# GpSimd writes and gathers scratch rows by index beside the experts of a cross-attention and mixture-of-experts layer

## The chip, the cores and the metric

One core of one Trainium2 chip. The metric is the time of the device for one execution in microseconds (us). Engines are named as in the profile: PE is TensorE (with PEld its weight loads), DVE VectorE, ACT ScalarE, POOL GpSimd, SP SyncE; a "q" behind a name is that engine's sequencer where it issues transfers.

## The reference, cut to what matters

Eight batches of 512 rows of 256 numbers go through two parts, each added to its input:

```python
x = x + xattn(ctx, layernorm(x), mask, ...)      # 8 heads of 32
x = x + ffn(layernorm(x), ...)
# ffn: 16 experts, the best 8 of a row by a gate, and a shared one
logits = l2norm(xf) @ l2norm(gate_w).T
combine = top-8 of sigmoid(logits), divided by their sum
y = (silu(xf @ w_gate[e]) * (xf @ w_up[e])) @ w_down[e]      # for each e
out = sum over e of combine[:, e] * y  +  (silu(xf @ sw_gate) * (xf @ sw_up)) @ sw_down
```

## The kernel before

The first part (attention) runs over 16 groups of 4 heads. The second part, which the change touches, runs over 8 x 17 units: for each batch b, the 16 experts e = 0 to 15 and the shared one as e = 16. All are computed for all rows. Numbers are split in a high and a low half, and each product is three matmuls.

**One order for all engines.** A list `ORDER` of steps is made before anything is built. Each engine's program walks the whole list and issues what is its own of each step, so the list is each engine's order; semaphores do the rest. The second part of the list is written by `order()`. For unit n = (b, e) it holds, in this order:

- in batch 0 only, `split_w` of a later expert (ACT rounds the weights to the high half at L866, POOL subtracts for the low half at L1429 and L1431). The weights of expert e + 2 are split ahead of unit e;
- `load_c`, which SP issues (L641): the combine weights of an expert, broadcast from a DRAM scratch to the tile `cb`, four buffers;
- `gate_up` (12 matmuls on PE), `silu` (ACT: `sg`), `unit` (DVE: `qb`, L1300 and L1311), `hi_h` (ACT: `hh`), `lo_h` (DVE: `hl`, L1316);
- what the next batch needs (below);
- `down` of unit n - 2 (6 matmuls on PE into `pst`).

**What the next batch needs.** At e = 0 to 6 of batch b five steps at a time of the chain `ln2` of batch b + 1 are put in. Its 33 steps are: statistics of the rows on DVE (steps 0 to 7: `st`, `mv`), two small ones on POOL (8 and 9: `ve`, L1358 and L1360), two on DVE (10 and 11: the first guess of a reciprocal root, L1067 and L1069), seventeen small ones on POOL (12 to 28, L1362 to L1378, the last writes `rn`), and four copies on ACT (29 to 32) that write the normalised rows into the tile `xm` (`XM`, 128 x 4 x 256). Step 29 lies at e = 5, steps 30 to 32 at e = 6. ACT waits ahead of step 29 until POOL has finished step 28. At e = 7 and e = 8 PE transposes `xm` (`turn_x2`, L665; four transposes each), and ACT and DVE split the result into the two halves that the units of batch b + 1 read. The gating follows at e = 10 to 13.

ACT, DVE and POOL run strictly in the list's order, so an ACT that waits at step 29 holds back the `silu` of unit e = 6 and all behind it. There is one `xm`.

In batch 0, POOL's splits of experts 9 to 16 fall beside units e = 7 to 14. PE's `gate_up` of an expert waits for its split.

Of the kernel before, what the change touches and what calls it, by code (L numbers as in the profile page):

```python
# [6 lines left out]
F32 = mybir.dt.float32  # L7
F32R = mybir.dt.float32r
I32 = mybir.dt.int32
# [4 lines left out]
B, S, D, F = 8, 512, 256, 512  # L14
# [34 lines left out]
N_TANH = 5  # L49


TODO = [(b, e) for b in range(B) for e in range(E + 1)]


# [180 lines left out]
def order():  # L235


    def chain(name, count, *key):
        return [(name, *key, i) for i in range(count)]

    out = attention()

    def run(c, k=None):
        k = len(c) if k is None else min(k, len(c))
        out.extend(c[:k])
        del c[:k]

    cb, split = FIRST_UNITS + NC, NEARLY
    turned = {0}
    tail = []  # L250

    def load_c(upto):
        nonlocal cb
        while cb < min(upto, B * E) and cb // E in turned:
            out.append(("load_c", cb))
            cb += 1

    c = []
    for n in range(FIRST_UNITS, len(TODO) + LAG):
        b, e = TODO[min(n, len(TODO) - 1)]  # L260
        if n < len(TODO):
            if b == 0:
                while split < min(e + 3, E + 1):
                    out.append(("split_w", split))
                    split += 1
            load_c(b * E + min(e, E) + NC)
            out += [("gate_up", n), ("silu", n), ("unit", n), ("hi_h", n), ("lo_h", n)]
            if b + 1 < B:
                if e == 0:
                    c = chain("ln2", N_LN2, b + 1)  # L270
                if e < 7:
                    run(c, 5)
                if e in (7, 8):
                    out.append(("turn_x2", b + 1, e - 7))
                if e == 10:
                    c = chain("gating", N_GATE, b + 1)
                if 10 <= e < 13:
                    run(c, 7)
                if e == 13:
                    run(c)  # L280
                    out.append(("turn_c", b + 1))
                    turned.add(b + 1)
            if tail and e in (3, 4):
                out.append(("store", tail[0], e - 3))
                if e == 4:
                    tail.pop(0)
        if n >= LAG:
            out.append(("down", n - LAG))
            if TODO[n - LAG][1] == E:
                tail.append(TODO[n - LAG][0])  # L290
    out += [("store", B - 1, 0), ("store", B - 1, 1)]
    return out


ORDER = order()


# [47 lines left out]

def build(nc, x, ctxT, mask, WsT, bs_k, bs_v, WtT, bt, WoT, bo, gate, wg, wu, wd, ident, out):
    cscr = nc.dram_tensor("combine_scratch", (B, 2 * E, 2, 4, 32), F32, kind="Internal").ap()
    with ExitStack() as top:
        made = {}

# [94 lines left out]
        assert place[0] + NEARLY * 24 * D <= late_at, "and these on the last group's"  # L445
        WX = s2("weights2", [128, E + 1, 6 * D], F32R)
        YT = s2("yt", [128, 2, S])
        OB = s2("ob", [128, 2, 2, D])
        GUh, GUl = (WX[:, :, 512 * n:512 * n + 512].rearrange("p e (a k h) -> p e a k h", a=2, k=2) for n in range(2))
        DNh, DNl = (WX[:, :, 1024 + D * n:1024 + D * n + D] for n in range(2))  # L450
# [101 lines left out]
        def sync_program(engine):  # L552
# [96 lines left out]
            for half in range(2):  # L649
                sp.wait_ge(sem(f"st_out{half}"), 16 * B)  # L650
            sp.wait_ge(sem("st_ct"), 64 * B)

        def tensor_program(engine):
            pe = Waiter(engine)
# [207 lines left out]
        def scalar_program(engine):  # L862
# [5 lines left out]
            for step in ORDER:  # L868
# [115 lines left out]
                elif step == ("grows", N_GROWS - 1):  # L984
                    act.wait_ge(sem("gate_t"), 1)
                    gb = bank(step)[:, 0:2 * E].rearrange("p (k e) -> p k e", k=2)
                    four = gb.rearrange("p k (f e) -> p k f e", f=1).to_broadcast([128, 2, 4, E])
                    copy(GT[:, :, :, 0, :], four).then_inc(sem("gate_hi"), 1)
                elif kind == "second_starts":
                    act.wait_ge(sem("ctx_lo"), 4 * B)  # L990
                    act.wait_ge(sem("q_lo"), NG)
                    act.wait_ge(sem("k_lo"), NG)
                    act.wait_ge(sem("v_f"), 2 * B)
                    act.wait_ge(sem("k"), NG)
                    act.wait_ge(sem("y_add"), COUNT["out_y", B - 1, 0, 1])
                    act.wait_ge(sem("x_bo"), B)
                elif kind in ("early_w", "split_w"):
                    e = step[1]
                    act.wait_ge(*w_loaded(e))
                    if FIRST_W <= e < NEARLY:  # L1000
                        act.wait_ge(*place_free(e))
                    copy(GUh[:, e].rearrange("p a k h -> p (a k) h"), WR[:, e % NR, 0:4, :]).then_inc(sem("w_hi"), 1)
                    copy(DNh[:, e, :], WR[:, e % NR, 4:6, :].rearrange("p a b -> p (a b)")).then_inc(sem("w_hi"), 1)
                elif kind == "ln2" and step[2] >= N_SMALL2:
                    _, b, i = step
                    q = i - N_SMALL2
                    act.wait_ge(sem("ln2"), N_SMALL2 * (b + 1))
                    if b > 0:
                        act.wait_ge(sem("x2_t"), 2 * b)
                    else:  # L1010
                        act.wait_ge(sem("x_t"), 2 * B)
                    copy(XM[:, q, :], X1[:, 4 * b + q, :], ACT.Identity, bias=NMR2[:, q:q + 1], scale=RS2[:, q:q + 1]).then_inc(
                        sem("xm"), 1)
                elif kind == "turn_x2":
                    _, b, j = step
                    act.wait_ge(sem("x2_t"), 2 * b + j + 1)
                    if b >= 2:
                        act.wait_ge(sem("gu"), 2 * 17 * (b - 1))
                    copy(X2h[:, b % 2, j, :], bank(step)).then_inc(sem("x2_hi"), 1)
                elif kind == "gating" and step[2] == N_TANH:  # L1020
                    b = step[1]
                    act.wait_ge(sem("gating"), N_GATE * b + 5)
                    act.wait_ge(sem("ln2"), N_SMALL2 * (b + 1))
                    for q in range(4):
                        copy(SC[:, q, :], LG[:, q, :], ACT.Tanh, scale=RN[:, q:q + 1]).then_inc(sem("tanh"), 1)
                elif kind == "first_ends":
                    act.wait_ge(sem("av"), 2 * NG)
                    act.wait_ge(sem("u_norm"), NG)
                    act.wait_ge(sem("y_add"), COUNT["out_y", B - 1, 1, 1])
                    act.wait_ge(sem("ut_lo"), NG)  # L1030
                elif kind == "silu":
                    n = step[1]
                    if n == 0:
                        for z in range(2):
                            for h in range(4):
                                act.wait_ge(sem(f"stack{z}{h}"), 96 * B)
                    act.wait_ge(sem("gu"), 2 * n + 1)
                    if n >= 2:
                        act.wait_ge(sem("hq"), n - 1)
                    if n < TANH_UNITS:  # L1040
                        copy(SG[:, n % 2, :], GP[n][0], ACT.Tanh, scale=0.5).then_inc(sem("silu"), 1)
                    else:
                        copy(SG[:, n % 2, :], GP[n][0], ACT.Silu).then_inc(sem("silu"), 1)
                elif kind == "hi_h":
                    n = step[1]
                    b, e = TODO[n]
                    if e < E:
                        act.wait_ge(sem("hc"), b * E + e + 1)
                    else:
                        act.wait_ge(sem("hq"), n + 1)  # L1050
                    if n >= NH:
                        act.wait_ge(sem("dn"), n - NH + 1)
                    copy(HHB[:, n % NH, :], QB[:, n % 2, :]).then_inc(sem("h_hi"), 1)
                elif kind == "down":
                    b, e = TODO[step[1]]
                    if e == E:
                        act.wait_ge(sem("dn"), step[1] + 1)
                        if b > 0:
                            act.wait_ge(sem("y_t"), 2 * b)
                        copy(YT[:, 0, :], YP[:, 0, :]).then_inc(sem("yt0"), 1)  # L1060

# [273 lines left out]
        def gpsimd_program(engine):  # L1335
            pool = Waiter(engine)

            for step in ORDER:
# [79 lines left out]
                elif kind == "second_starts":  # L1418
                    pool.wait_ge(sem("k"), NG)
                    pool.wait_ge(sem("v_f"), 2 * B)  # L1420
                    pool.wait_ge(sem("y_add"), COUNT["out_y", B - 1, 0, 1])
                elif kind in ("early_w", "split_w"):
                    e, i = step[1], W_AT[step[1]] - 1
                    if FIRST_W <= e < NEARLY:
# [51 lines left out]
```

## Time and profile before

| | |
|---|---|
| median of 2 runs | 1054.62 us (1053.51 to 1055.73) |
| the profiled execution's own time | 1049.61 us |
| its span in the profile | 1047.5 us |
| PE busy | 1003.0 us (96%) |
| DVE busy | 655.4 us (63%) |
| ACT busy | 467.2 us (45%) |
| POOL busy | 389.4 us (37%) |
| DMA, mean | 84 GB/s |

The first part and the second meet between 430 and 475 us; from there on the profile is eight times the same stretch. A share of busy time of the whole span mixes both. The times of one batch are read from the timeline, where two equal instructions of two batches lie a batch apart.

### The profile page before, as it was taken

Reading aid. Unit: us, or ns where it says so; the run is one execution under the profiler, and the core shown is the slowest. Engines: PE = TensorE matmul, PEld = TensorE weight load, DVE = VectorE, ACT = ScalarE, POOL = GpSimd, SP = SyncE. Lnnn points to the kernel's source line nnn. Section 1 sums busy time; section 2 is a strip of 40 time slices with the busy share of each in tenths; the row PEclk is TensorE's granted clock in tenths of the full one; section 3 lists DMA queues with packets and bytes.
Section 4 is the critical chain, followed back from the end, with each engine's and each line's share of the span. In section 5 each row is a group of like instructions: output and inputs, shape, how many; then the busy total and the mean of one; then the engine's idle time right before and its main releaser. Section 6 shows DMA issues by size and latency. Waiting matters only on the chain.

```text
span 1047.5 us, 14744 instructions
## 1 busy us (share of the span) xinstructions
PE 1003.0 (96%) x5070; PEld 761.4 (73%) x5070; DVE 655.4 (63%) x1510; ACT 467.2 (45%) x881; POOL 389.4 (37%) x355
## 2 busy tenths in 40 slices
PE   4889999999999998899999999999999999999998
PEld 3656767676767664567888888888888888888886
DVE  6866767776767577445665566556556556555544
ACT  3447565666565646445424333333333333333322
POOL 2569797879797967345310010010010100100000
PEclk9999999999999997999999999999999999999999
DMA  7543342424242223325333232242341232332230
GB/s 232 131 132 93 101 132 67 128 72 134 70 114 70 65 64 101 81 81 122 95 72 68 52 81 58 54 82 50 63 80 42 71 82 46 74 75 60 67 72 24
DMA packets 84377, 87.87 MB, mean 84 GB/s; under 512 B 13160, under 2 KB 66296, under 8 KB 84304
## 3 DMA queue, kind: packets, MB, share of 16 engines
q1 hardware_dynamic: 82384, 84.85, 32.9%
q10 hardware_dynamic: 1920, 2.10, 0.6%
q8 instruction: 40, 0.66, 0.3%
q14 instruction: 33, 0.27, 0.1%
HBM read 56.99 MB, written 4.46 MB: 59 GB/s over the span
## 4 chain that ended last, share of the span: by engine, by line
PE 89%; DVE 5%; ACT 2%; SPq 1%; issue 1%; POOL 1%; DMA 1%; DVEq 0%; ACTq 0%; POOLq 0%
PE ps L659 49%; PE pst L659 18%; PE ps L765 5%; PE ps L738 5%; PE pst L754 5%; PE ps L665 4%; DVE mx L1196 1%; PE ps L778 1%; SPq L611 1%; SPq L546 1%; ACT e_buf L866 1%; DVE lg L1277 1%; ACT ctx_h L866 0%; DVE wsrc_l L1145 0%; DMA x<-in_x 0%
## 5 line engine op out<-in xcount | busy, mean ns | idle before, releaser
L659 PE MATMUL ps<-x_h,weights 128*128 128x512 f32 x1088 | 365.6, 397 | 2.8 <-DVE sg L1297 2.0
L659 PEld LDWEIGHTS ps<-x_h,weights 128*128 128x128 f32 x1088 | 204.4, 188 | 52.7 <-issue 2.5
L1196 DVE TENSOR_REDUCE mx<-ps 128x1 f32<-128x512 f32 x256 | 173.2, 684 | 95.4 <-PE ps L738 94.8
L659 PE MATMUL ps<-x_l,weights 128*128 128x512 f32 x544 | 214.5, 394 | 0.0
L866 ACT ACTIVATE hh<-qb 128x512 fp32r<-128x512 f32 x136 | 86.0, 632 | 287.7 <-DVE qb L1311 268.2
L659 PE MATMUL pst<-hh,weights 128*128 128x512 f32 x544 | 193.2, 397 | 0.0
L866 ACT ACTIVATE e_buf<-pst 128x512 f32<-128x512 f32 x256 | 147.1, 595 | 100.4 <-PE pst L754 90.5
L1300 DVE TENSOR_TENSOR qb<-ps,sg 128x512 f32<-128x512 f32 x136 | 94.0, 691 | 135.9 <-PE ps L659 132.2
L1316 DVE TENSOR_TENSOR hl<-qb,hh 128x512 fp32r<-128x512 f32 x136 | 94.3, 693 | 92.2 <-ACT hh L866 92.0
L1406 POOL TENSOR_TENSOR e_sums<-e_sums,e_buf 128x1024 f32<-128x1024 f32 x60 | 143.4, 2390 | 8.6 <-ACT e_buf L866 2.5
L1358 POOL TENSOR_SCALAR ve<-mv 128x4 f32<-128x4 f32 x8 | 1.8, 229 | 337.8 <-DVE mv L1238 337.8
L738 PE MATMUL ps<-k_stack,q_stack 97*128 97x512 f32 x256 | 109.8, 431 | 11.3 <-DVE mx L1196 9.1
L659 PEld LDWEIGHTS ps<-x_l,weights 128*128 128x128 f32 x544 | 102.1, 188 | 24.9
L659 PEld LDWEIGHTS pst<-hh,weights 128*128 128x128 f32 x544 | 102.1, 188 | 24.0 <-DVE hl L1316 0.8
L754 PE MATMUL pst<-q_stack,k_stack 98*128 98x512 f32 x256 | 108.2, 424 | 10.3 <-ACT e_buf L866 10.2
L866 ACT ACTIVATE sg<-ps 128x512 f32<-128x512 f32 x136 | 80.9, 595 | 74.6 <-PE ps L659 73.6
L659 PE MATMUL pst<-hl,weights 128*128 128x512 f32 x272 | 107.5, 395 | 0.0
L1406 POOL TENSOR_TENSOR e_sums<-e_buf 128x1024 f32<-128x1024 f32 x30 | 71.8, 2395 | 50.3 <-PE ps L778 50.0
L1311 DVE TENSOR_TENSOR qb<-qb,cb 128x512 f32<-128x512 f32 x124 | 87.8, 708 | 4.2
L738 PEld LDWEIGHTS ps<-k_stack,q_stack 97*128 97x128 f32 x256 | 49.2, 193 | 52.4 <-issue 32.3
L754 PEld LDWEIGHTS pst<-q_stack,k_stack 98*128 98x128 f32 x256 | 49.3, 193 | 25.5 <-ACT e_buf L866 17.3
L765 PE MATMUL ps<-e_buf,v_buf 128*32 128x512 f32 x512 | 65.1, 628 | 0.0
(154 smaller groups left out, 1360.7 us busy)
## 6 DMA issues: line engine op xcount, KB each, us to landing
cb<-combine_scratch SPq DMA_DIRECT2D x128, 256.0 KB, 4.7
q_stack<-q_h SPq DMA_DIRECT2D x128, 64.0 KB, 2.0
k_stack<-k_h SPq DMA_DIRECT2D x124, 64.0 KB, 2.0
ctx_raw<-in_ctxT SPq DMA_DIRECT2D x7, 1024.0 KB, 5.3
q_stack<-q_l SPq DMA_DIRECT2D x64, 64.0 KB, 2.0
out_x<-ob SPq DMA_DIRECT2D x16, 256.0 KB, 2.1
k_stack<-k_l SPq DMA_DIRECT2D x62, 64.0 KB, 2.0
x<-in_x SPq DMA_DIRECT2D x7, 512.0 KB, 6.8
```

The lines of the kernel that those rows point to most:

```text
L546: e.dma_start(f32(KS[g % 2][at:at + 32, h, :]), f32(src[32 * h:32 * h + 32, :])).then_inc(sem(f"stack{g % 2}{h}"), 16)
L659: ins = engine.matmul(dst, lhsT, rhs, start=start and n == 0, stop=stop and n == len(terms) - 1)
L665: ins = engine.transpose(dst, src, ID[0:k, 0:k])
L738: engine.matmul(ps, QS[z][0:97, h, 128 * q:128 * q + 128], KS[z][0:97, h, :], start=True, stop=True).then_inc(sem("s_max"), 1)
L754: engine.matmul(YP[:, m % 2, :], KS[z][0:98, h, 128 * k:128 * k + 128], QS[z][0:98, h, :], start=True, stop=True).then_inc(sem("s_t"), 1)
L765: ins = engine.matmul(OP[32 * i:32 * i + 32, :], VB[:, b % 2, k, hh + i, :], EB[:, SLOTS[8 * g + 4 * (i // 2) + k], i % 2, :], start=k == ...
L866: return engine.activation(dst, src, func, **kw)
L1196: engine.tensor_reduce(MX[:, g % 2, h // 2, h % 2, q:q + 1], bank(step), AX.X, ALU.max).then_inc(sem("max"), 1)
L1300: engine.tensor_tensor(QB[:, w, :], GP[n][1], SG[:, w, :], ALU.mult).then_inc(sem("hq"), 1)
L1311: engine.tensor_tensor(QB[:, w, :], QB[:, w, :], CB[:, m % NC, :], ALU.mult).then_inc(sem("hc"), 1)
L1316: engine.tensor_tensor(HLB[:, n % NH, :], QB[:, w, :], f32(HHB[:, n % NH, :]), ALU.subtract).then_inc(sem("h_lo"), 1)
L1406: engine.tensor_tensor(ES[:, a, :, :], first, EB[:, SLOTS[n + 1 + i], :, :], ALU.add).then_inc(sem("e_add"), 1)
```

## The change

A DRAM scratch `routed_rows` of 4096 rows of 256 numbers, a tile `ix` with the row numbers (partition p, column c holds 32 p + c) and a tile `gathered` with four buffers are added. POOL gets two kinds of steps:

- `put`: 32 for each batch b + 1, at e = 6 to 13 of batch b, four in each unit. Each is an indirect DMA that writes 128 rows of `xm` (1 KB each) to the scratch rows named by a column of `ix`; each of the four quarters of `xm` is written eight times. The first waits for the four copies into `xm` and, from the second batch on, until all 32 gathers before have landed.
- `take`: 32 for each batch from 1 on, at e = 0 to 5 of that batch, 6, 5, 5, 6, 5 and 5 of them, behind the `ln2` steps of the same e. Each is an indirect DMA that gathers 128 rows from the scratch into `gathered`. The first waits until all 32 puts have landed; each waits until the take four before it has landed, since it writes the same buffer.

Nobody reads `gathered`. ACT gets one more wait, ahead of step 29: the puts of the batch before must have landed, since the copies write `xm` again. SP waits for the last takes at the end. The 7 batches 1 to 7 have 224 puts and 224 takes in all.

```diff
+PUTS = 32
...
+            if b + 1 < B and 6 <= e < 14:
+                out += [("put", b + 1, 4 * (e - 6) + i) for i in range(4)]
+            if b > 0 and 0 <= e < 6:
+                out += [("take", b, i) for i in range(PUTS) if i * 6 // PUTS == e]
...
+    routed = nc.dram_tensor("routed_rows", (128 * PUTS, D), F32, kind="Internal").ap()
...
+        IX, GB = s2("ix", [128, PUTS], I32), s2("gathered", [128, 4, D])
...
+            for i in range(4):
+                sp.wait_ge(sem(f"take{i}"), 16 * 8 * (B - 1))
...
                     act.wait_ge(sem("ln2"), N_SMALL2 * (b + 1))
+                    if b > 1:
+                        act.wait_ge(sem("put"), 16 * PUTS * (b - 1))
...
+                elif kind == "put":
+                    _, b, c = step
+                    if (b, c) == (1, 0):
+                        pool.wait_ge(sem("dn"), 1)
+                        engine.iota(IX[:, :], pattern=[[1, PUTS]], base=0, channel_multiplier=PUTS).then_inc(sem("ix"), 1)
+                        pool.wait_ge(sem("ix"), 1)
+                    if c == 0:
+                        pool.wait_ge(sem("xm"), 4 * (b + 1))
+                        if b > 1:
+                            for i in range(4):
+                                pool.wait_ge(sem(f"take{i}"), 16 * 8 * (b - 1))
+                    engine.indirect_dma_start(routed, bass.IndirectOffsetOnAxis(IX[:, c:c + 1], 0), XM[:, c // 8, :], None).then_inc(
+                        sem("put"), 16)
+                elif kind == "take":
+                    _, b, c = step
+                    pool.wait_ge(sem("put"), 16 * PUTS * b)
+                    if b > 1 or c >= 4:
+                        pool.wait_ge(sem(f"take{c % 4}"), 16 * (8 * (b - 1) + c // 4))
+                    engine.indirect_dma_start(GB[:, c % 4, :], None, routed, bass.IndirectOffsetOnAxis(IX[:, c:c + 1], 0)).then_inc(
+                        sem(f"take{c % 4}"), 16)
```

POOL's order before, in a batch's chain `ln2`, its first six small steps (`rs`, `rs_a` and `rs_b` are the root's small tiles, `ve` the variances; in brackets the semaphores waited for):

```order
L1358 TENSOR_SCALAR ve<-mv 128x4 [waits xm,tanh,ln2]
L1360 TENSOR_SCALAR ve<-mv 128x4 [waits ln2]
L1362 TENSOR_TENSOR rs_a<-rs 128x8 [waits ln2]
L1364 TENSOR_TENSOR rs_b<-rs_a,ve 128x8 [waits ln2]
L1366 TENSOR_SCALAR rs_b<-rs_b 128x8 [waits ln2]
L1368 TENSOR_TENSOR rs<-rs,rs_b 128x8 [waits ln2]
```

The same place in the changed kernel, batch 1 (its lines stand 11 to 31 further down):

```order
L1369 TENSOR_SCALAR ve<-mv 128x4 [waits tanh,ln2]
L1371 TENSOR_SCALAR ve<-mv 128x4 [waits ln2]
L1451 DMA gathered<-routed_rows,ix 128x256 [waits take2]
L1451 DMA gathered<-routed_rows,ix 128x256 [waits take3]
L1451 DMA gathered<-routed_rows,ix 128x256 [waits take0]
L1451 DMA gathered<-routed_rows,ix 128x256 [waits take1]
L1451 DMA gathered<-routed_rows,ix 128x256 [waits take2]
L1373 TENSOR_TENSOR rs_a<-rs 128x8 [waits ln2]
L1375 TENSOR_TENSOR rs_b<-rs_a,ve 128x8 [waits ln2]
L1377 TENSOR_SCALAR rs_b<-rs_b 128x8 [waits ln2]
L1451 DMA gathered<-routed_rows,ix 128x256 [waits take3]
```

Five takes stand between the first two small steps and the next three; 5, 6 and 5 more stand between the later groups, 21 in all from `ve` to `rn`.

POOL's order before, at the splits of batch 0 (`weights` is the tile with all experts' halves, `w_raw` the loaded weights):

```order
L1429 TENSOR_TENSOR weights_65<-w_raw,weights_65 128x512 [waits w_hi]
L1431 TENSOR_TENSOR weights_65<-w_raw,weights_65 128x256 [waits w_hi]
L1429 TENSOR_TENSOR weights_65<-w_raw,weights_65 128x512 [waits w_hi]
L1431 TENSOR_TENSOR weights_65<-w_raw,weights_65 128x256 [waits w_hi]
L1429 TENSOR_TENSOR weights_65<-w_raw,weights_65 128x512 [waits w_hi]
```

The same place in the changed kernel, from the split of expert 8 to that of expert 10:

```order
L1462 TENSOR_TENSOR weights_65<-w_raw,weights_65 128x256 [waits w_hi]
L1437 IOTA ix 128x32 [waits dn]
L1444 DMA routed_rows<-xm,ix 4096x256 [waits xm,ix]
L1444 DMA routed_rows<-xm,ix 4096x256 x3
L1460 TENSOR_TENSOR weights_65<-w_raw,weights_65 128x512 [waits w_hi]
L1462 TENSOR_TENSOR weights_65<-w_raw,weights_65 128x256 [waits w_hi]
L1444 DMA routed_rows<-xm,ix 4096x256 x4
L1460 TENSOR_TENSOR weights_65<-w_raw,weights_65 128x512 [waits w_hi]
```

Four puts now stand ahead of each of the splits of experts 9 to 16, 32 in all. From batch 1 on the 32 puts stand together on POOL.

## Rows read from the trace of the kernel before

**Rows 1.** The page: busy time by engine; busy tenths, clock and DMA in 40 slices

```profile
PE 1003.0 (96%) x5070; PEld 761.4 (73%) x5070; DVE 655.4 (63%) x1510; ACT 467.2 (45%) x881; POOL 389.4 (37%) x355
...
PE   4889999999999998899999999999999999999998
...
POOL 2569797879797967345310010010010100100000
```

**Rows 2.** Busy time in four stretches of one batch each, all engines

```profile
core 0: us, PE busy (x) PEld busy (x) DVE busy (x) ACT busy (x) POOL busy (x), PEclk, DMA share, GB/s
538.00:612.00 74.00, 74.00 (x328) 59.77 (x327) 43.27 (x91) 25.06 (x46) 4.82 (x20) 1.00 0.31 65
612.00:686.00 74.00, 74.00 (x328) 59.84 (x327) 43.27 (x91) 25.07 (x46) 4.85 (x20) 1.00 0.27 65
```

**Rows 3.** Timeline of POOL, chain ln2 beside batch 2: start, us, instruction, [idle before]

```profile
607.70 0.23 POOL L1358 TENSOR_SCALAR ve<-mv 128x4 f32<-128x4 f32 x1 [64.15 <-DVE mv L1238]
608.01 0.24 POOL L1360 TENSOR_SCALAR ve<-mv 128x4 f32<-128x4 f32 x1
611.88 0.20 POOL L1362 TENSOR_TENSOR rs_a<-rs 128x8 f32<-128x8 f32 x1 [3.63 <-DVE rs L1069]
...
617.28 0.24 POOL L1378 TENSOR_SCALAR rn<-v 128x4 f32<-128x4 f32 x1
681.64 0.23 POOL L1358 TENSOR_SCALAR ve<-mv 128x4 f32<-128x4 f32 x1 [64.12 <-DVE mv L1238]
```

**Rows 4.** Timeline of ACT, the same batch, at e = 5 and 6

```profile
624.11 0.59 ACT L866 ACTIVATE xm<-x,nmr,rs 128x256 f32<-128x256 f32 x1
624.92 0.60 ACT L866 ACTIVATE sg<-ps 128x512 f32<-128x512 f32 x1 [0.22 <-PE ps L659]
...
628.31 1.57 ACT L866 ACTIVATE xm<-x,nmr,rs 128x256 f32<-128x256 f32 x3
```

**Rows 5.** Timeline of PE: the transposes of xm, and where expert 16 of batch 0 begins

```profile
630.32 0.60 PE L665 MATMUL ps<-ident_sb,xm 128*128 128x128 f32 x4
...
519.15 0.40 PE L659 MATMUL ps<-x_h,weights 128*128 128x512 f32 x1
```

**Rows 6.** Timeline of POOL, batch 0: the splits of experts 8 (second half), 9 and 16

```profile
480.12 1.19 POOL L1431 TENSOR_TENSOR weights<-w_raw,weights 128x256 fp32r<-128x256 f32 x1
481.98 1.28 POOL L1429 TENSOR_TENSOR weights<-w_raw,weights 128x512 fp32r<-128x512 f32 x1 [0.66 <-ACT weights L866]
...
515.79 0.75 POOL L1431 TENSOR_TENSOR weights<-w_raw,weights 128x256 fp32r<-128x256 f32 x1
```

**Rows 7.** Groups of POOL by shape, whole run: busy, mean ns, idle before

```profile
L1406 POOL TENSOR_TENSOR e_sums<-e_sums,e_buf 128x1024 f32<-128x1024 f32 x60 | 143.4, 2390 | 8.6 <-ACT e_buf L866 2.5
L1429 POOL TENSOR_TENSOR weights<-w_raw,weights 128x512 fp32r<-128x512 f32 x17 | 21.9, 1287 | 48.5 <-ACT weights L866 48.5
L1431 POOL TENSOR_TENSOR weights<-w_raw,weights 128x256 fp32r<-128x256 f32 x17 | 13.4, 791 | 0.0
```

**Rows 8.** Instructions on the tile cb: SP's issues, ns min, median, max

```profile
L641 SPq DMA_DIRECT2D cb<-combine_scratch x128: 359/360/1393, 425.9 to 1018.5; - x128
```

**Rows 9.** The page: DMA queue of SP, and issues with KB each and us to landing

```profile
q1 hardware_dynamic: 82384, 84.85, 32.9%
...
cb<-combine_scratch SPq DMA_DIRECT2D x128, 256.0 KB, 4.7
...
w_raw<-in_wg SPq DMA_DIRECT2D x17, 128.0 KB, 2.2
```

**Rows 10.** Busy time in stretches of 5 us where PE waits for others

```profile
390.00:395.00 5.00, 3.65 (x17) 2.10 (x15) 2.21 (x5) 3.25 (x7) 4.26 (x11) 0.90 0.38 92
395.00:400.00 5.00, 4.22 (x14) 3.14 (x14) 2.53 (x4) 3.38 (x8) 2.45 (x2) 0.50 0.43 110
```

**Rows 11.** Timelines of POOL and DVE, the same moment

```profile
615.01 0.74 POOL L1366 TENSOR_SCALAR rs_b<-rs_b 128x8 f32<-128x8 f32 x1
...
615.00 0.69 DVE L1316 TENSOR_TENSOR hl<-qb,hh 128x512 fp32r<-128x512 f32 x1 [0.70 <-ACT hh L866]
```

## The prediction

> **What bounds the kernel now.** I read the page's busy times first. PE is busy for 96% of the span and POOL for 37%, but the slices show that POOL's work lies in the first half: from slice 20 on its row reads mostly 0 and 1, and PE's reads 9 but for its last slice [rows 1]. The change lies in that second half, so the mean over the span says nothing of it. The stretches of one batch each do: 74 us long, PE busy for all 74.00, DVE for 43.3, ACT for 25.1, POOL for 4.8 [rows 2]. So one batch is limited by PE alone, and POOL has 69 us of it free. On the share of busy time the change looks free. The timeline has to say whether it is, since POOL's 4.8 us are not just any 4.8 us: they lie in a chain that PE waits for if it is late.
>
> That chain: POOL begins `ve` at 607.70, waits for DVE's first guess until 611.88, and ends `rn` at 617.52. The next batch's `ve` begins at 681.64, so a batch takes 73.94 us [rows 3]. ACT comes to the first copy into `xm` at 624.11, 6.6 us after `rn`: this is all the slack that the chain has. ACT's other three copies end at 629.88 [rows 4], and PE transposes `xm` from 630.32 on [rows 5], 0.44 us later. PE takes its work in order, so every microsecond that `xm` is late beyond that is a microsecond without matmuls.
>
> **What the change puts there.** Nothing is removed. Added are 224 puts and 224 takes, all issued by POOL, 64 in each of the six batches 1 to 6, 32 puts in batch 0 and 32 takes in batch 7. Everything depends on c, the time for which one indirect DMA of 128 rows occupies POOL. The trace of before has no transfer issued by POOL, so c has to be bounded. From below: SP issues a transfer of 256 KB in 0.36 us [rows 8], with nothing but its sequencer at work. From above: a POOL instruction over 128 x 1024 elements, 2.39 us; nearer by are the splits over 128 x 256 and 128 x 512, 0.79 and 1.29 us [rows 7]. [...] I take 1.15 us, between the two splits and nearer to the larger. Below 0.36 us or below nothing I see no reason for it to go: nothing that POOL did before goes away.
>
> *The chain ln2 beside batches 1 to 6.* By the order, 21 takes stand between `ve` and `rn`. POOL's two `ve` end 0.55 us after the start, the 17 small steps take 5.64 us (611.88 to 617.52) [rows 3], and the wait for DVE (3.63 us) is filled by the first five takes if c is over 0.73. So `rn` ends 6.2 + 21c after `ve` began. It may end up to 624.11 - 607.70 = 16.4 us after, and 0.44 us more for PE's slack and some 0.2 for ACT's idle time before `sg` [rows 4, 5]: 17.0. PE loses 21c - 10.8 in each batch; with c = 1.15 that is 13.35, six times 80 us.
>
> *POOL's own round.* In the same batches POOL has 6.2 + 64c, and twice it must wait for landings: the puts for the last take, the takes for the last put. A transfer of 128 KB lands 2.2 us after its issue [rows 9]. 64 x 1.15 + 6.2 + 4.4 = 84.2 us, against 73.9 + 13.35 = 87.3 by the chain. The chain is the longer until c = 1.2; above it POOL sets the pace, with a loss of 64c - 63.3 a batch.
>
> *Batch 0.* Four puts stand ahead of each split of experts 9 to 16. POOL is free at 481.3 (480.12 + 1.19), iota costs some 0.3 and the eight splits 8 x 2.03 (1.28 + 0.75), so that the last ends at 497.8 + 32c. It ended at 516.5 before [rows 6], and PE begins expert 16 at 519.15 [rows 5]. PE loses 32c - 21.3, with c = 1.15 15.5 us. SP, which waits there for POOL's `w_lo` before it loads weights and then `cb`, is behind by the same and not by more.
>
> [...]
>
> *DMA.* The 64 transfers of a batch move 8192 rows of 1 KB. SP's queue had 82384 packets of about 1 KB, which took 32.9% of 16 engines for 1047.5 us, 67 ns each [rows 9]: 8192 x 67 ns / 16 = 34 us a batch, 46% beside the 27 to 31% of before [rows 2]. That stays under 100%, and `cb` is loaded four units ahead of its use (17 us) while it lands in 4.7 [rows 9]. I cost it at nothing; if that cover goes, DVE's `qb` waits. ACT's new wait for the puts is nothing, since POOL gathered after they had landed. The wait of SP at the end is nothing: the takes of batch 7 end 40 us before it.
>
> *POOL beside DVE.* At 615.01 a small step of POOL takes 0.74 us, where its like take 0.20 to 0.24; DVE's subtraction with two inputs in SBUF runs from 615.00 to 615.69 [rows 11]. An indirect DMA that reads `ix` may be held up in the same way. I count this as part of c, since nothing shows it for a transfer. [...]
>
> The row of POOL's splits speaks for a c over 1 us. [...]
>
> Sum: 80 + 15.5 + 15 = 110.5 us on the profiled execution's 1049.6, hence 1160. The median of before lies 5 us above that execution; the same 5 us give 1165.
>
> **Rivals.**
>
> 1. *POOL is occupied for longer and becomes the bound* (c over 1.2). For it: POOL's compute over 1024 elements takes 2.39 us [rows 7], and DVE holds POOL up at times [rows 11]. With c = 1.45: 6 x 29.5 + 25 + 15 = 217 us, 1272. With the upper bound 2.39: 6 x 89.7 + 55 + 15, about 1660. The batch then follows POOL's round and POOL is busy nearly all the time.
>
> 2. *No change: POOL only hands the transfer on.* If c is near SP's 0.36 [rows 8], 21 takes go into the chain's slack. The ring of four buffers then sets their pace: (0.36 + 2.2) / 4 = 0.64 us a take, 13.4 + 6.2 = 19.6 against 17.0, and with the clock left alone a loss of 2.6 x 6 = 16 us, 1070; with landings in 1.5 us nothing, 1055. It decides at c = 0.7 (0.6 us a take is about the slack). Against it: an index must be read for each row. [...]
>
> 3. *The landings set the pace.* If a gather lands as late as `cb` does, 4.7 us [rows 9], a take costs (c + 4.7) / 4 = 1.46 us whatever the engine does: 21 x 1.46 - 10.8 = 19.9 a batch, 120 + 15.5 + 15, 1205. For it: three times the traffic, and writes 32 KB apart. Against it: 128 KB loads of weights land in 2.2.
>
> 4. *The DMA engines fill.* If a scattered row cost twice the 67 ns, 68 + 22 = 90 us a batch, and 6 x 16 = 96 us more, much the same time as forecast with other waits (`cb` late, DVE waiting on DMA).
>
> **Chances.** Forecast (c from 0.75 to 1.2, PE waits for the transposes of `xm`): 0.50. Rival 1: 0.25. Rival 2: 0.12. Rivals 3 and 4: 0.08 and 0.05. The forecast's own range is 1090 (c = 0.75: 6 x 5 + 3 + 3) to 1180. To hold the time 8 times in 10 it reaches down to 1080 and, for rival 1 up to c = 1.45, to 1270. A measurement tells about 2% from no change, 21 us. Under it lie most of rival 2 and a little beside: 0.13. Faster needs a cause, and there is none in the change: 0.01. Slower: 0.86.
>
> **What would show it.** In the profile after: 448 indirect DMAs on POOL, spaced 1.15 us apart where 32 puts stand together; `ve` to `rn` some 30 us instead of 9.8; PE idle some 13 us once a batch ahead of the transposes of `xm`, with ACT waiting for POOL's `rn` ahead of its copy; granted clock of 0.5 for some us after it; a batch of about 87 us in place of 73.9; and PE waiting on `weights` in batch 0 from expert 11 or so on. Wrong would be: a spacing under 0.7 or over 1.3, a `ve` that waits for POOL's own queue rather than for DVE, takes that wait for their buffer, or DVE waiting for `cb`.

## The result, and the profile after

The changed kernel takes 1197.16 us (1196.82 to 1197.51), the kernel before 1054.62 us: a ratio of 1.137, with a 95% interval of 1.133 to 1.141. The profiled execution is one of the two, 1196.82 us, with a span of 1195.0 us; against that of before it is 147.2 us longer, 4.7 more than the medians are apart (142.5), because the profiled execution of before was a quick one. Some executions of a kernel take longer at a lower granted clock; such ones are left out of every comparison, and below only the kernel with half the count and late takes has any (two of four, 1086.1 and 1097.0 us, at 0.972 and 0.970 against 0.981 for the other two).

First the page of the kernel after, as [rows 1] and [rows 9]: busy times, three of the slice rows, and SP's and POOL's DMA queues.

```profile
PE 1027.9 (86%) x5070; PEld 779.0 (65%) x5070; DVE 661.8 (55%) x1510; ACT 467.9 (39%) x881; POOL 842.9 (71%) x804
...
PE   5889999999999889879599679859949939949998
...
POOL 2669778797797734886767767767767667767760
PEclk9899999999999899889889879979969979969999
...
q1 hardware_dynamic: 82384, 84.85, 30.5%
q0 software_dynamic: 21504, 58.75, 14.4%
```

PE's row has a dip once per batch from slice 19 (counted from 0) on, and the clock is lower in the same slices. PE's busy time rose by only 25 us, so most of the 147 is idle time. Which wait that is, the view of waits says (total us, times, longest us), here for the kernel after:

```profile
ACT xm L875 <- POOL rn L1389: 118.3, 8, 19.9
PE ps L674 <- ACT xm L875: 106.6, 6, 18.4
POOL routed_rows L1444 <- DMA gathered<-routed_rows,ix: 20.2, 6, 3.5
PE ps L668 <- POOL weights L1462: 15.3, 7, 3.5
POOL gathered L1451 <- DMA gathered<-routed_rows,ix: 12.4, 19, 2.5
POOL gathered L1451 <- DMA routed_rows<-xm,ix: 10.3, 6, 1.7
POOL ve L1369 <- DVE mv L1249: 7.3, 1, 7.3
```

PE waits six times for the transposed copy `xm`, ACT waits ahead of it for POOL's `rn`, and in batch 0 PE waits for `weights`. The last line is the one to stop at: POOL waits for DVE's `mv` once, where each `ve` of before waited 64 us for it [rows 3]. From the second batch on nothing holds POOL but its own queue and the landings of its own transfers. Its timeline shows that directly: start, us, instruction, idle time before it with what ended it.

```profile
657.09 0.60 POOL L1369 TENSOR_SCALAR ve<-mv 128x4 f32<-128x4 f32 x1
...
665.81 1.53 POOL L1451 DMA_INDIRECT gathered<-routed_rows,ix  x1 [0.15 <-issue]
667.64 0.95 POOL L1451 DMA_INDIRECT gathered<-routed_rows,ix  x1 [0.31 <-issue]
...
689.96 0.24 POOL L1389 TENSOR_SCALAR rn<-v 128x4 f32<-128x4 f32 x1
...
699.93 1.01 POOL L1444 DMA_INDIRECT routed_rows<-xm,ix  x1 [3.39 <-DMA gathered<-routed_rows,ix]
701.25 0.98 POOL L1444 DMA_INDIRECT routed_rows<-xm,ix  x1 [0.30 <-issue]
...
740.95 0.97 POOL L1444 DMA_INDIRECT routed_rows<-xm,ix  x1 [0.30 <-issue]
743.62 0.99 POOL L1451 DMA_INDIRECT gathered<-routed_rows,ix  x1 [1.70 <-DMA routed_rows<-xm,ix]
...
750.93 0.53 POOL L1369 TENSOR_SCALAR ve<-mv 128x4 f32<-128x4 f32 x1
```

One indirect DMA executes for 0.97 us and the next begins 0.30 us later, put down to `issue`: 1.27 us from start to start in a train of puts, 1.25 in one of takes. That, and not the 0.95, is the c of the prediction. The two gaps of 3.39 and 1.70 us are the landings at the two turns between takes and puts. From one `ve` to the next it is 750.93 - 657.09 = 93.8 us, before it was 73.9.

The issues of the puts in the kernel after (the last number is the median us from issue to landing; the takes have the same 3.6), and the busy time of all engines in that batch, as [rows 2]:

```profile
routed_rows<-xm,ix POOLq DMA_INDIRECT x224, 3.6
```

```profile
657.09:751.50 94.41, 75.99 (x324) 61.12 (x324) 43.31 (x91) 24.46 (x45) 69.35 (x84) 0.89 0.50 140
```

POOL is "busy" for 69.35 of 94.41 us there although it never rests: the 0.30 us between two issues count as idle (64 x 0.30 = 19 us), and the rest are the two landings. A POOL at 73% is here the bound. PE is busy for 2 us more than in [rows 2], at a clock of 0.89, and idle for 18.

### The profile page after: what moved, and what is told of

It reads as the page before. It is cut to its first block, busy times and chain, and to the rows that moved or that the text cites. A ratio compares the mean times of both kernels' runs of the same rounds, so it can differ in the third digit from the quotient of the medians.

```text
span 1195.0 us, 15214 instructions
## 1 busy us (share of the span) xinstructions
PE 1027.9 (86%) x5070; PEld 779.0 (65%) x5070; DVE 661.8 (55%) x1510; ACT 467.9 (39%) x881; POOL 842.9 (71%) x804
## 3 DMA queue, kind: packets, MB, share of 16 engines
q0 software_dynamic: 21504, 58.75, 14.4%
## 4 chain that ended last, share of the span: by engine, by line
PE 41%; POOL 34%; issue 11%; DMA 6%; DVE 4%; ACT 2%; SPq 1%; DVEq 0%; POOLq 0%; ACTq 0%
PE ps L668 20%; POOL routed_rows L1444 16%; POOL gathered L1451 13%; PE ps L774 5%; PE ps L747 5%; PE pst L763 4%; PE pst L668 4%; DMA gathered<-routed_rows,ix 4%; PE ps L674 2%; DVE mx L1207 1%; PE ps L787 1%; POOL weights L1460 1%; DMA routed_rows<-xm,ix 1%; POOL weights L1462 1%; SPq L618 1%
## 5 line engine op out<-in xcount | busy, mean ns | idle before, releaser
L668 PE MATMUL ps<-x_h,weights 128*128 128x512 f32 x1088 | 373.4, 404 | 18.1 <-POOL weights L1462 15.3
L1444 POOL DMA_INDIRECT routed_rows<-xm,ix x224 | 231.2, 1032 | 85.6 <-issue 65.2
L1451 POOL DMA_INDIRECT gathered<-routed_rows,ix x224 | 219.3, 979 | 82.8 <-issue 58.4
L668 PEld LDWEIGHTS ps<-x_h,weights 128*128 128x128 f32 x1088 | 209.4, 192 | 72.3 <-POOL weights L1462 18.3
L668 PE MATMUL ps<-x_l,weights 128*128 128x512 f32 x544 | 218.5, 402 | 0.0
L668 PE MATMUL pst<-hh,weights 128*128 128x512 f32 x544 | 199.5, 409 | 0.0
L668 PEld LDWEIGHTS pst<-hh,weights 128*128 128x128 f32 x544 | 106.2, 195 | 25.1 <-DVE hl L1327 0.8
L668 PE MATMUL pst<-hl,weights 128*128 128x512 f32 x272 | 110.5, 406 | 0.0
L674 PE MATMUL ps<-ident_sb,xm 128*128 128x128 f32 x64 | 13.6, 352 | 106.6 <-ACT xm L875 106.6
L1322 DVE TENSOR_TENSOR qb<-qb,cb 128x512 f32<-128x512 f32 x124 | 91.4, 737 | 4.2
```

The costliest lines, as they stand in the source:

```text
L668: ins = engine.matmul(dst, lhsT, rhs, start=start and n == 0, stop=stop and n == len(terms) - 1)
L1322: engine.tensor_tensor(QB[:, w, :], QB[:, w, :], CB[:, m % NC, :], ALU.mult).then_inc(sem("hc"), 1)
L1444: engine.indirect_dma_start(routed, bass.IndirectOffsetOnAxis(IX[:, c:c + 1], 0), XM[:, c // 8, :], None).then_inc(sem("put"), 16)
L1451: engine.indirect_dma_start(GB[:, c % 4, :], None, routed, bass.IndirectOffsetOnAxis(IX[:, c:c + 1], 0)).then_inc(sem(f"take{c % 4}"), 16)
```

## The experiments

Each is made from the kernel after, but for the one with SP's transfers, which is made from the kernel before. Of the edits the lines that matter are shown. Ratios are against the kernel before, run on the same chip (1053.8 to 1054.3 us).

**Each half alone.** The puts without the takes:

```diff
-            if b > 0 and 0 <= e < 6:
-                out += [("take", b, i) for i in range(PUTS) if i * 6 // PUTS == e]
```

> All 224 puts stay where they are, the takes are left out (nothing of the reference's computation is changed). Theory R, POOL's round (in a steady batch POOL needs 64 issues at 1.27 us each, its ln2 steps and two landings, 94.6 us, and PE follows it): 32 issues are 41 us a batch and fit beside PE's 73.9; only batch 0 loses, 32 x 1.27 - 21.3 = 19 us: about 1075 us. Theory C, the chain (21 takes between ve and rn are what PE waits for, whatever the round): the same 1075, since no take is left in the chain. Theory D, the traffic on the DMA engines or the landings slow the units: half the traffic stays, so about half of the 142 us stays: 1120 to 1130, with DVE waiting for cb.

Measured: 1076.9 us, ratio 1.024 (1.021 to 1.028). Waits of PE and POOL in this kernel:

```profile
PE ps L665 <- POOL weights L1458: 16.5, 7, 3.5
...
POOL routed_rows L1440 <- ACT xm L872: 75.9, 6, 12.7
```

The batches are at 73.95 us, as before, and POOL waits for others in each, for up to 12.7 us ahead of the puts alone. What is left, 23 us, is batch 0: PE waits 16.5 us in all for the splits of the experts, and between these waits it works at a granted clock of 0.89 (from 484 to 562 us), where the kernel before has 1.00.

The takes, with the puts of batch 1 alone left in, so that the batches 2 to 6 gather the same rows again:

```diff
-            if b + 1 < B and 6 <= e < 14:
+            if b == 0 and 6 <= e < 14:
```

> All 224 takes stay, but of the puts only the 32 of batch 1; later takes gather the same scratch rows. Theory R: the round of a batch has 32 issues, 41 us, and fits; only batch 0 loses 19 us: 1075 us. Theory C: in each of six batches rn is late, 21 x 1.27 - 10.8 = 16 us, 95 us, with batch 0 and some time at the lower clock 1170 to 1185 us. Theory D: about 1125 us.

Measured: 1190.3 us, ratio 1.131 (1.127 to 1.134), though 192 of the 448 transfers are gone. Timeline of POOL:

```profile
657.30 0.23 POOL L1369 TENSOR_SCALAR ve<-mv 128x4 f32<-128x4 f32 x1 [42.86 <-DVE mv L1249]
...
691.76 0.24 POOL L1389 TENSOR_SCALAR rn<-v 128x4 f32<-128x4 f32 x1
749.72 0.23 POOL L1369 TENSOR_SCALAR ve<-mv 128x4 f32<-128x4 f32 x1 [42.86 <-DVE mv L1249]
```

POOL is idle for 43 us of each batch, and the batch still takes 92.4 us. So its total is not needed for the loss: 21 takes between `ve` and `rn`, 34.7 us instead of 9.8, are enough. (34.7 - 17.0 gives 17.7 of the 18.5 us a batch; the clock, 0.91 in this batch, may be the rest.)

**The other way round: the chain free, the total kept.** All 32 takes of a batch at e = 6, behind `rn` and ahead of the puts:

```diff
+            if b > 0 and e == 6:
+                out += [("take", b, i) for i in range(PUTS)]
```

> The same 448 transfers, but the 32 takes of a batch stand together at e = 6, behind rn and ahead of the next puts; no take stands between ve and rn. Theory R: POOL's round is as long as before (64 x 1.27 + 9.8 + a landing = 94.7 us): 1190 to 1200 us, as the changed kernel. Theory C: the chain is free, only batch 0 loses: 1075 us. If both hold, each being enough alone, the time stays near 1195.

Measured: 1220.8 us, ratio 1.161 (1.158 to 1.164). `rn` ends 7.8 us after `ve`, PE's wait for `xm` is down to 2.7 us in all, and the batch takes 102.3 us, the others 98 to 101. That is 20 us above the upper end of what was expected. Waits in this kernel:

```profile
DVE rs_a L1078 <- POOL ve L1371: 149.6, 6, 33.4
PE ps L668 <- DVE qb L1311: 108.3, 5, 25.3
...
POOL gathered L1451 <- DMA gathered<-routed_rows,ix: 30.1, 36, 2.2
```

Nothing is in the chain any more, but POOL comes to `ve` some 25 us late, since 64 transfers and their landings take longer than a batch. With the takes in one block the ring of four buffers holds them up as well (for 30.1 us in all, 12.4 in the kernel after), and the turn to the puts costs up to 7.2 us. So POOL's round alone is enough, too, and moving all takes out of the chain made the kernel 24 us slower. The change meets two limits of nearly the same size, and removing one shows the other.

**Is it POOL's time or the traffic?** In place of each transfer, an addition on POOL over 128 x 512 elements, which [rows 7] have at 1.29 us; no added byte moves:

```diff
-                    engine.indirect_dma_start(GB[:, c % 4, :], None, routed, ...
+                    engine.tensor_tensor(GB[:, 0:2, :], GB[:, 0:2, :], GB[:, 2:4, :], ALU.add)
```

> Every put and take is replaced, at its place, by an addition on POOL over 128 x 512 elements of the tile gathered (1.24 us from one to the next, up to 1.3 with its wait), no transfer is issued by POOL and no landing is waited for. Theories R and C, POOL's time alone matters: six batches of 89 to 90 us by the chain and the round alike, batch 0 20 us: 1165 to 1185 us. Theory D: the traffic is gone, 1055 to 1065 us.

Measured: 1252.2 us, ratio 1.190 (1.187 to 1.194), and PE waits for `xm` six times, for 124.4 us in all. The groups of these additions (count, busy us, mean ns, idle before):

```profile
L1440 POOL TENSOR_TENSOR gathered<-gathered 128x512 f32<-128x512 f32 x224 | 332.3, 1484 | 17.4
L1444 POOL TENSOR_TENSOR gathered<-gathered 128x512 f32<-128x512 f32 x224 | 317.2, 1416 | 16.1
```

POOL time without traffic is enough for the loss. It is 70 us above the expectation: an addition took 1.42 to 1.48 us on average, not the 1.29 of the splits, and a batch 103 us. The stand-in is not a clean one, since it holds up DVE as well: DVE's multiplication by `cb` took 1.16 us on average (0.71 before) and its subtraction `hl` 1.05 (0.69 before). DVE is still busy for only 62 of the 103 us, POOL for 97.

The reverse, the same bytes without POOL: SP issues them as plain transfers, 8 puts and 8 takes of 512 KB a batch, at the same experts.

```diff
+                    engine.dma_start(routed[512 * i:512 * i + 512, :].rearrange("(q p) d -> p q d", p=128), XM[:, :, :])
```

> The same bytes in the same stretches, written and read back in 8 + 8 plain transfers of 512 KB a batch issued by SP; POOL issues none. If POOL's time is the whole cost, 1053 to 1062 us. If DMA engines or HBM traffic cost, DVE waits for cb (SP stands at the landings of the new transfers, up to 10 us each, against 12 us of cover that cb has): 1070 to 1110.

Measured: 1053.4 us, ratio 0.9985 (0.9963 to 1.0006). The 448 x 128 KB cost nothing here, although the transfers and `cb` now share SP's queue:

```profile
q1 hardware_dynamic: 141520, 143.58, 50.2%
...
cb<-combine_scratch SPq DMA_DIRECT2D x128, 256.0 KB, 5.9
routed_rows<-xm SPq DMA_DIRECT2D x56, 512.0 KB, 6.8
```

`cb` lands in 5.9 us instead of 4.7 [rows 9], still far inside its four units. What this leaves out is the index, and rows that lie 32 KB apart; the kernel after had both, at a DMA share of 0.50, and no wait of PE or DVE in the second part is put down to a DMA.

**What the index costs.** POOL issues the same 448 transfers, but plain, so that the 128 rows of each also lie side by side in the scratch:

```diff
+                    engine.dma_start(routed[128 * c:128 * c + 128, :], XM[:, c // 8, :])
```

> The same 448 transfers of 128 rows issued by POOL at the same places, but as plain ones without an index. Two limits: with a spacing s between two issues, the round is 64 s + 13.4 and the chain 73.9 + 21 s - 10.8. If the index is what costs, s falls to 0.6 or less and the time to 1055 to 1070 us; if writing the descriptors does (128 rows either way), s stays at 1.1 to 1.27 and the time at 1160 to 1197.

Measured: 1115.0 us, ratio 1.059 (1.055 to 1.063). Groups of this kernel:

```profile
L1450 POOL DMA_DIRECT2D gathered<-routed_rows x224 | 123.4, 555 | 106.6 <-DMA gathered<-routed_rows 69.1 <-DMA routed_rows<-xm 31.7 <-issue 4.7
L1444 POOL DMA_DIRECT2D routed_rows<-xm x224 | 119.5, 542 | 32.5 <-DMA gathered<-routed_rows 31.2 <-issue 0.9 <-POOL ix L1437 0.3
```

```profile
656.66 16.99 POOL L1444 DMA_DIRECT2D routed_rows<-xm  x32 [5.35 <-DMA gathered<-routed_rows]
```

A plain transfer occupies POOL for 0.55 us, and the 0.30 us behind it are gone: 32 puts in a train take 16.99 us. The indexed form takes more than twice that. Which part of the difference is the reading of the index and which the scattered rows, this run can't say, since it takes away both. The time missed its expectation (1055 to 1070 us), which left out the ring of buffers: at 0.55 it paces the takes (69 us of waits for their buffer, a landing of 3.0 us). (0.55 + 3.0) / 4 = 0.89 us a take gives a chain of 24.9 us, measured were 25.0 to 26.6, and PE still waits 46 us for `xm`. This is rival 2's mechanism, with plain transfers.

**The size of one transfer.** The puts alone, with 64 of the 128 rows each (`IX[0:64, ...]`, `XM[0:64, ...]`); and the puts alone, 16 a batch, with rows of 2 KB (`XM[:, 2 * (c // 8):2 * (c // 8) + 2, :]`), so that half as many carry all bytes:

> As puts_only (224 puts, no takes), but each put writes 64 rows of the tile xm in place of 128; nothing of the reference is changed. If an issue costs by the row, the spacing of the puts falls from 1.27 to 0.65 us or so; if it is fixed, it stays at 1.2 to 1.27. Between them: a fixed part and a part by the row.

> As puts_only, but 16 puts a batch of 128 rows of 2 KB each (two quarters of xm side by side), so the same bytes in half the issues. If an issue costs by rows or is fixed, the spacing stays 1.27 us and batch 0 loses 1 to 5 us: about 1055 us. If it costs by bytes, the spacing doubles and the time is that of puts_only, 1077.

Measured in one execution each: 1232.2 us and 1058.7 us. Groups and timeline, 2 KB rows first, then 64 rows:

```profile
L1440 POOL DMA_INDIRECT routed_rows<-xm,ix x112 | 115.4, 1030 | 107.3 <-ACT xm L872 76.0 <-issue 31.0 <-POOL ix L1434 0.3
```

```profile
599.29 0.89 POOL L1440 DMA_INDIRECT routed_rows<-xm,ix  x1 [0.30 <-issue]
```

The mean is 1.03 us for rows of 1 KB and of 2 KB, so twice the bytes in a row made no difference here. With half of the rows it is 1.20 from start to start against 1.27: 64 rows more cost 0.07, and by an estimate from these two points about 1.13 us are there whatever the rows. With 64 and with 128 rows an indirect DMA took POOL nearly the same time here, and fewer, wider ones are the remedy: 16 wide puts cost 5 us where 32 cost 23. (The 5 are from one execution, and those of the kernel before lie between 1048.8 and 1056.2 us; the 18 between the two are clear of that.) The kernel with 64 rows is far slower than any theory had it; the last experiments are about that.

**Half the count.** `PUTS = 16`, two puts per unit:

> 16 puts and 16 takes a batch, two puts in each unit, 3, 3, 2, 3, 3 and 2 takes at e = 0 to 5, so 11 between ve and rn. POOL's round is 32 x 1.27 + 13.4 = 54 us and no bound any more. Theory of two limits (the batch takes the longer of POOL's round and of the chain): rn ends 6.2 + 11 x 1.33 = 20.8 us after ve began, 3.8 us later than the 17.0 that PE allows, six times, and 1 to 5 us in batch 0: 1075 to 1095 us, with PE idle 3 to 5 us ahead of the transposes of xm. Theory of the round alone: 1055 to 1060.

Measured: 1080.6 us, ratio 1.027 (1.021 to 1.033). Timeline of POOL:

```profile
612.33 0.22 POOL L1369 TENSOR_SCALAR ve<-mv 128x4 f32<-128x4 f32 x1 [25.09 <-DVE mv L1249]
...
631.73 0.24 POOL L1389 TENSOR_SCALAR rn<-v 128x4 f32<-128x4 f32 x1
```

The chain takes 19.6 us, 2.6 over the 17.0 of the prediction's deadline, and the batch 76.6 instead of 73.9 (the next ones 75.8 to 76.0). The deadline is at the right place. It does not account for all of the 26 us: from the last `ve` to the end of the span are 161.8 us, 17.8 more than before, and in that stretch, from 960 to 990 us, PE is idle for 8 us with no wait for `xm`, at a granted clock that falls to 0.50. These are the pauses of the last experiments.

The same with the takes behind `rn` (at e = 6), so that neither limit is met:

> 16 puts and 16 takes a batch, all takes at e = 6 behind rn. Neither the round (54 us) nor the chain (9.8 us) is late: 1053 to 1062 us, all transfers hidden but for batch 0. [...]

Measured: 1069.9 and 1084.4 us. Both are above what was expected. In the second of them the batches take 74.6 to 80.5 us, PE's wait for `xm` is gone, and in its place stand a wait for DVE and pauses that belong to no wait:

```profile
PE pst L668 <- DVE yt L1335: 7.4, 2, 7.2
...
PE pst L668 <- issue: 7.3, 11, 1.0
...
PE ps L668 <- issue: 2.6, 6, 1.0
```

**Pauses that no wait explains.** They are much larger in the kernel with 64 rows. Its waits, a piece of PE's timeline during the puts, and the busy times of that stretch:

```profile
PE ps L665 <- issue: 76.0, 36, 3.6
...
PE pst L665 <- issue: 45.0, 34, 3.0
```

```profile
614.84 0.58 PE L665 MATMUL ps<-x_h,weights 128*128 128x512 f32 x1 [2.22 <-issue]
617.64 0.58 PE L665 MATMUL ps<-x_l,weights 128*128 128x512 f32 x1 [2.22 <-issue]
```

```profile
600.00:620.00 20.00, 5.92 (x17) 3.34 (x16) 0.00 (x0) 0.60 (x1) 14.82 (x18) 0.67 0.24 55
```

PE issues a matmul every 2.8 us with nothing that it waits for, DVE does nothing for 20 us, and the DMA engines are busy for a quarter. POOL alone runs on as usual, with a put every 1.20 us and 14.82 of the 20 us busy. One theory was that transfers pile up, since nothing limits how many puts are under way. The test: at most four, in this kernel and in the one with half the count and late takes.

```diff
+                    if b > 1 or c >= 4:
+                        pool.wait_ge(sem(f"put{c % 4}"), 4 * PUTS * (b - 1) + 16 * (c // 4))
```

> As rows64, but each put waits until the put four before it has landed, so that no more than four are under way. In rows64 PE was idle for 121 us for no semaphore's sake (issue), with matmuls up to 2.8 us apart while the puts ran. Theory Q (transfers pile up, and what the engines' own instruction supply needs stands behind them): with four under way the idle time of PE from issue falls below 15 us and the time to 1075 to 1100 us; POOL then shows the slow landings. Theory F (the form of a 64-row transfer or its issue disturbs the other engines in itself): the idle time from issue and 1232 us stay.

> As half_late, but each put waits until the put four before it has landed (the takes do so already). half_late had PE idle for 10 us from issue and 7 us behind DVE, in the stretch in which its 16 puts follow each other, and took 1070 to 1097 us. Theory Q: 1054 to 1065 us and no idle time of PE from issue. Theory F: 1070 to 1097 us as before.

Measured: 1204.9 us, ratio 1.143 (1.140 to 1.146), and 1079.9 us, ratio 1.023 (1.019 to 1.027, which leaves open whether it is 2% slower). With 64 rows, 65.8 + 19.7 us of such pauses are left of 121; with half the count they stay about as they were (8.8 + 4.5 us against 7.3 + 2.6).

The limit hardly ever made a put wait (7 of 224 puts for 4.9 us in all, and 4 of 112 for 2.1), and the pauses stayed: piled-up transfers are not the cause, or not most of it. What it is stays open. In the kernel after the change there are none on the matmuls of the experts, so the result doesn't hang on it.

## Why the prediction came out as it did

The time lay in its range, and its model of two limits, the chain and POOL's round, held. Which of them binds came out the other way than forecast: rival 1 came true (c above 1.2, POOL's round as the bound), which had a quarter of the chance, and 1197 us lie above the forecast's own 1180. One of its signs of being wrong showed, a `ve` that waits for POOL's own queue and not for DVE. The forecast was 32 us short because c was mis-sized, more than because of the switch: the takes alone, where the chain binds, took 1190 us.

- **c.** Taken as 1.15 us, measured 1.27. This is the term that was mis-sized. Between the bounds of 0.36 and 2.39 the choice was good, but it was a choice between two rows on other instructions, so that it came within a tenth is partly luck, and this tenth is counted 384 times in the six batches. With the rows it hardly goes: halving them takes off 0.07 us. That 0.30 of the 1.27 us would lie behind the instruction, and not in it, was not foreseen.
- **The chain.** Predicted 30 us from `ve` to `rn` and a deadline of 17.0; the kernel after took 33.1, the takes alone 34.7. The form 21c - 10.8 is near: with 1.27 it gives 15.9, and the takes alone lost 18.5 in a batch.
- **POOL's round.** The form 64c - 63.3 assumed landings of 2.2 us; they took 3.6. With c = 1.27 it gives 18.0 a batch. Measured were 93.8 - 73.9 = 19.9: the two turns account for 5.1 us instead of 4.4, and transfers that fall beside operations of DVE, by an estimate, for more (the takes were 0.03 us and the puts 0.06 us above their medians on average, up to 1.53 us in one). Above the crossing at c = 1.2 this is the longer one, as the missing wait for `mv` shows. Six such batches are 119 us of the 142.5 between the medians. POOL was "busy nearly all the time", as rival 1 has it, only if the 0.30 us are counted in.
- **Batch 0.** Predicted 15.5 us; the puts alone cost 23. With 1.27 the formula gives 19.3. The rest is in operations of POOL and DVE that meet. First the splits' second halves as a group in the kernel after, as in [rows 7], then the timelines of POOL and DVE in the kernel after, at expert 16, and of POOL at the first put behind the split of expert 9 (the next puts have 0.96):

```profile
L1462 POOL TENSOR_TENSOR weights<-w_raw,weights 128x256 fp32r<-128x256 f32 x17 | 16.9, 992 | 0.0
```

```profile
544.85 1.23 POOL L1462 TENSOR_TENSOR weights<-w_raw,weights 128x256 fp32r<-128x256 f32 x1
...
543.74 1.77 DVE L1322 TENSOR_TENSOR qb<-qb,cb 128x512 f32<-128x512 f32 x1
```

```profile
492.34 1.50 POOL L1444 DMA_INDIRECT routed_rows<-xm,ix  x1 [0.16 <-issue]
```

  A mean of 0.992 us against 0.791, 17 times, is 3.4 us. It lies in seven of the eight late splits, which now fall beside DVE's multiplication by `cb` (five) or its subtraction `hl` (two), each with 1.21 to 1.24 us, where the one other late split has 0.75. DVE's operation is longer too in six of the seven, 0.95 to 2.20 us: this one has 1.77, where the kernel before has 0.69 for DVE's two-input subtraction [rows 11]. The first put behind a split is stretched as well, to 1.25 to 1.51 us behind six of the eight, 3.0 us in all. Against that a split follows its last put without the 0.30 us, which by an estimate gives back one to two. 19.3 + 3.4 + 3.0 - 1.5 is 24.2, about the 23 measured.
- **The clock.** 15 us were added to the sum. No run shows this term; what the runs showed in its place is a clock that did fall: the stretches of 6 us around one of the waits, in the kernel after (columns as in [rows 2]), show 0.50 and 0.58 granted, and then 1.00 again. By an estimate from these means that is 0.50 for about 11 of the 18 us, in which PE had work for about five; half of these is 2.5 us a batch, and PE's busy time is 2.0 us higher in the batch shown above.

```profile
594.00:600.00 6.00, 0.00 (x0) 0.00 (x0) 2.08 (x3) 3.02 (x6) 4.54 (x9) 0.50 0.29 90
600.00:606.00 6.00, 5.78 (x18) 4.72 (x19) 2.67 (x4) 1.86 (x5) 2.15 (x3) 0.58 0.58 135
606.00:612.00 6.00, 6.00 (x30) 4.88 (x29) 2.74 (x5) 2.22 (x4) 4.48 (x6) 1.00 0.35 97
```

  In the regime that came about it adds nothing, because PE ends its work and then waits for POOL anyway; 119 + 23 are 142, which is all that the medians are apart.
- **DMA at nothing.** Right, as SP's plain transfers show for the bytes, and for the scattered rows the missing waits in the kernel after. The share of the DMA engines rose by some 20 points (0.50 against 0.27 to 0.31), not by 46: the queue of POOL has 21504 packets for 448 x 128 = 57344 rows, 2.7 rows in each.
- **POOL beside DVE.** The take at 665.81 lasted 1.53 us instead of 0.95, beside DVE's subtraction `hl` at 665.73. With the additions on POOL, of the splits' shape, the mean was 1.42 to 1.48 us against 1.29. POOL's plain transfers were hardly held up (none of their 224 takes lasted over 0.65 us, none of the puts over 0.79). The prediction counted this inside c, and it is little there: over their medians of 0.95 and 0.97 us the takes and the puts were 0.03 and 0.06 longer on average.
- **The other rivals.** Rival 2 (POOL only hands on) fell: 1.27 is far from its 0.7. (Its threshold was set too high: the slack of 10.8 us over 21 takes is 0.51 us a take, not 0.6 or 0.7, and with 0.55 us and the ring PE did wait, 46 us.) Rival 3 (landings set the pace) fell too: takes waited for their buffer for 12.4 us in all, though landings were 3.6. Rival 4 (the DMA engines fill) fell with a DMA share of 0.50.

## What to carry to other kernels

Price an instruction by its spacing from start to start in a train, not by its busy time: here the gap of 0.30 us behind each indirect DMA made an engine that looked 73% busy the bound. When work is added to an engine that is mostly idle, make two sums, one for the chain of small steps that others wait for and one for its whole round, and expect the loss of the larger (with c = 1.27 they gave 15.9 and 18.0 us a batch here, and 19.9 were lost); moving the work away from the chain helps only while the round still fits (here it made 1221 us of 1197). An indirect DMA cost GpSimd 1.2 to 1.3 us here, with 64 or 128 rows and with 1 or 2 KB in each, so wider rows and fewer calls come first, and transfers whose addresses are known belong on another queue (SP's cost nothing here, GpSimd's plain ones 6%).

## What was not expected of the hardware

- An indirect DMA occupied POOL for 1.27 us with 128 rows of 1 KB, the same mean busy time (1.03 us) with rows of 2 KB, and 1.20 us with 64 rows. A plain DMA issued by POOL took 0.55 us.
- Scatter puts on 64 of 128 partitions brought PE pauses of 121 us with no wait behind them, matmuls 2.8 us apart at a DMA share of 0.24, and 155 us more than the same number of puts with twice the rows (one execution). At most four transfers under way left 85 us of them. The cause is open.
- Where GpSimd's additions (1.42 to 1.48 us) took the place of the transfers, DVE's operations with two inputs in SBUF took 1.05 to 1.16 us on average instead of 0.69 to 0.71.
- The same bytes, 58.7 MB more, cost nothing measurable beside the matmuls when SP issued them in plain transfers of 512 KB (1053.4 us, ratio 0.9985).
